# Work moved around the first attention's way through DRAM in a four-layer attention kernel: norms, constants, a late unit and a rounding, with fewer idle products and the fourth layer's constants on ScalarE

## The reference

```python
# layer 0: linear attention over 1500 keys, 16 heads; then layernorm(att @ dense_w + dense_b)
kv = einsum('bhnd,bhne->bhde', k_prime, vh); att = (q' kv) / (q' . sum k')
# ffn 0: quantised (8 bit rows, three-valued weights) silu(gate) * up, down
# layer 1: windowed attention (the 56 first keys, rotary positions), mixture of 16+2 experts
# layer 2: k = l2norm(layernorm(ctx) @ Wk) * k_scale; attention of normalised queries over 1556 keys, 8 heads
#          quantised gelu ffn
# layer 3: attention over 1500 keys, 16 heads, softmax with a row maximum; mixture of 8 experts
```

## Time and profile before

| | |
|---|---|
| three runs, median (lowest to highest) | 840.04 us (837.87 to 840.55) |
| the profiled execution's own time | 838.38 us |
| its span | 836.6 us, mean granted TensorE clock 0.943 |
| PE busy | 747.0 us, 89% of the span |
| DVE busy | 605.0 us, 72% |
| ACT busy | 416.7 us, 50% |
| POOL busy | 321.8 us, 38% |
| chain that ended last | PE 47%, DVE 37%, ACT 5%, POOL 5% |

### The profile page before, as it was taken

The page is one execution under the profiler, slowest core; times in us unless marked ns, Lnnn a source line. Parts: engine busy times, 40 slices in busy tenths (PEclk is TensorE's granted clock), DMA queues, the critical chain, the costliest instruction groups (busy, mean ns, idle before and its releaser), DMA issues.

```text
span 836.6 us, 15735 instructions
## 1 busy us (share of the span) xinstructions
PE 747.0 (89%) x5624; PEld 490.0 (59%) x5624; DVE 605.0 (72%) x1279; ACT 416.7 (50%) x694; POOL 321.8 (38%) x263
## 2 busy tenths in 40 slices
PE   4699999997876969998999999997799998998997
PEld 3577777875544565653455555563246665655575
DVE  4789999998887665557556665568789997535653
ACT  2666666676664524435554545411137776834331
POOL 0665555551423602530778777721251211100111
PEclk9999999999988868999999999998869999998999
DMA  7266766432415312216033322027715667000320
GB/s 204 74 211 244 256 215 214 167 117 94 76 50 175 118 35 81 81 39 165 2 91 108 107 77 77 0 30 109 157 54 107 129 143 151 3 1 26 112 77 24
DMA packets 50338, 87.84 MB, mean 105 GB/s; under 512 B 17386, under 2 KB 34730, under 8 KB 49922
## 3 DMA queue, kind: packets, MB, share of 16 engines
q1 hardware_dynamic: 50274, 86.98, 38.0%
HBM read 61.45 MB, written 25.51 MB: 104 GB/s over the span
## 4 chain that ended last, share of the span: by engine, by line
PE 47%; DVE 37%; ACT 5%; POOL 5%; issue 4%; DMA 1%; SPq 0%; DVEq 0%; POOLq 0%; ACTq 0%
DVE arena L2414 9%; PE ps L1145 8%; PE ps L1135 6%; DVE arena L1810 6%; DVE rn L1962 5%; PE ps L1313 3%; PE ps L1066 3%; DVE arena L2011 3%; PE ps L1323 3%; DVE arena L1990 2%; PE ps L1250 2%; PE ps L750 2%; PE ps L1239 2%; PE ps L1079 2%; DVE arena L1970 2%
## 5 line engine op out<-in xcount | busy, mean ns | idle before, releaser
L1810 DVE TENSOR_TENSOR arena<-ps,arena 128x448 f32<-128x448 f32 (+7 forms) x139 | 82.4, 617 | 57.1 <-ACT arena L1622 20.9
L2414 DVE TENSOR_REDUCE arena<-ps 112x1 f32<-112x500 f32 x192 | 114.6, 669 | 8.8 <-PE ps L1222 8.7
L1747 POOL TENSOR_TENSOR arena<-arena 125x448 f32<-125x448 f32 x96 | 109.2, 1138 | 24.6 <-ACT arena L1567 20.8
L1145 PE MATMUL ps<-arena 125*128 125x448 f32 (+1 forms) x208 | 97.2, 548 | 2.0 <-ACT arena L1567 1.5
L1598 ACT ACTIVATE arena<-ps 125x896 f32<-125x896 f32 x96 | 87.2, 917 | 22.7 <-PE ps L1239 22.7
L1567 ACT ACTIVATE arena<-arena,kbias 125x448 f32<-125x448 f32 x96 | 63.6, 668 | 65.4 <-DVE arena L1810 47.9
L1810 DVE TENSOR_TENSOR arena<-ps,rn 125x448 f32<-125x448 f32 x96 | 59.2, 618 | 48.8 <-PE ps L1135 43.9
L1135 PE MATMUL ps<-arena 128*125 128x448 f16 (+3 forms) x312 | 76.6, 354 | 0.1
L825 PE MATMUL ps<-w_k2h,arena 128*125 128x512 f16 x288 | 67.6, 386 | 8.5 <-ACT arena L1379 8.5
L1135 PEld LDWEIGHTS ps<-arena 128*125 128x125 f16 (+1 forms) x312 | 40.3, 133 | 53.7 <-issue 42.3
L1725 POOL TENSOR_TENSOR arena<-arena 112x512 f32<-112x512 f32 x23 | 29.1, 1267 | 88.9 <-DVE arena L1810 88.7
(11 more groups left out here) (310 smaller groups left out, 1413.8 us busy)
## 6 DMA issues: line engine op xcount, KB each, us to landing
arena<-in_ctxT SPq DMA_DIRECT2D x8, 750.0 KB, 9.4
d_cln<-arena SPq DMA_DIRECT2D x8, 750.0 KB
d_clnT<-arena SPq DMA_DIRECT2D x8, 750.0 KB
d_k<-arena SPq DMA_DIRECT2D x24, 250.0 KB
d_v<-arena SPq DMA_DIRECT2D x24, 250.0 KB
arena<-d_clnT SPq DMA_DIRECT2D x8, 750.0 KB
arena<-in_ctx SPq DMA_DIRECT2D x8, 672.0 KB
arena<-d_cln SPq DMA_DIRECT2D x8, 672.0 KB
```

Of the source, the lines that this page charges most:

```text
L1145: pe.matmul(ps[0:D, 4 + 2 * p, 0:N], cln_s[p][0:rows, t, :], pexp[(t + p) % 2][0:rows], start=(t == 0), stop=(t == KT)).then_inc(l2_pv, 1)
L1747: ins = pool.tensor_tensor(psum2[p][0:rows], psum2[p][0:rows], pexp[(t + p) % 2][0:rows], ALU.add)
L1810: return dve.tensor_tensor(out, a, b, op)
L2414: dve.tensor_reduce(mx3[bn % 2][:, u % 2, u % 8 // 2, u // 8:u // 8 + 1], ps[0:TT, max_bank_of(bn, u), 0:500], AX.X, ALU.max).then_inc(l3_ ...
```

## The change

It moves work, drops some idle products and gives one set of constants to another engine:

- **ScalarE:** unit 10 and `k1T` are taken before the wait for the store; then the squares of ten key tiles and of two more, then the constants, then unit 11, then the last six squares. The root of the norms goes behind units 17 and 18.
- **GpSimd:** multiplies `k1T` by the cosines and adds the sines' part (VectorE makes that part alone), between units 10 and 11; the first two `key_blocks` go behind the first two powers, with a wait for the store instead of `l1_zero`.
- **TensorE:** unit 11 goes behind the projection and two of the key tiles; six tiles remain behind it. A wait for `l1_zero` stands before the first scores.
- **VectorE:** four norms of the last sequence before the turn instead of six, the weights' rounding under the projection, two norms under the second layernorm's power, three and one around the first ffn, two under the queries' product; the clamp `rn_sq` and `key_biases` under the rotation.
- **SyncE:** the wait for `rn_sq` and the loads of units 20 to 23 go from before unit 16's store to unit 19's.
- **Idle products:** 26 become 22 in the second ffn, 14 become 7 and 12 become 6 in the third layer's start.
- **Third layer's start:** the latent keys' sums of squares are made in four pieces, three of them before the copies of the turned queries; their reciprocal goes behind four of the eight subtractions.
- **Fourth layer:** ScalarE sets `v3s` after the third attention (two fills by Identity with scale 0, four small copies) instead of GpSimd's memsets.

```diff
@@ sync
-            sp.wait_ge(rn_sq, 1)
-            for u in range(20, 24):
-                load_later(u)
             for u in range(16, 24):
+                if u == 19:
+                    sp.wait_ge(rn_sq, 1)
+                    for v in range(20, 24):
+                        load_later(v)
                 store_later(u)
@@ tensor
-            later(11)
             pe.wait_ge(l0_att, 3)
             l2_keys(B - 1, 0, 8, range(KT // 2, KT), bank=3)
-            l2_keys(B, 1, 0, range(KT // 2), bank=3)
+            l2_keys(B, 1, 0, range(4), bank=3)
             pe.wait_ge(l0_ld, 32)
             transposes(y2, 2)
             op.next()
             by_tokens(xT2, w_d0[:, :], 0)
-            l2_keys(B, 1, 0, range(KT // 2, KT), bank=3)
+            l2_keys(B, 1, 0, range(4, 6), bank=3)
+            later(11)
+            l2_keys(B, 1, 0, range(6, KT), bank=3)
...
-                    keep_clock(26, 7)
+                    keep_clock(22, 7)
...
+            pe.wait_ge(l1_zero, 3)
             scores1(0)
...
-            keep_clock(14, 3)
+            keep_clock(7, 3)
...
-            keep_clock(12, 2)
+            keep_clock(6, 2)
@@ scalar
+            later(10)
+            act.wait_ge(l1_kv, 1)
+            act.activation(k1T, ps[0:D, 1, 0:N], ACT.Identity, bias=w_col1[:, 1:2]).then_inc(l1_ak, 1)
+            l2_squares(B - 1, 8, range(KT // 2, KT), bank=3)
+            l2_squares(B, 0, range(6), bank=3)
             for p in range(2):
                 act.wait_ge(st[p], 32 * (B // 2 + 1))
...
-            later(10)
-            act.wait_ge(l1_kv, 1)
-            act.activation(k1T, ps[0:D, 1, 0:N], ACT.Identity, bias=w_col1[:, 1:2]).then_inc(l1_ak, 1)
             later(11)
-            l2_squares(B - 1, 8, range(KT // 2, KT), bank=3)
-            l2_squares(B, 0, bank=3)
+            l2_squares(B, 0, range(6, KT), bank=3)
...
+            later(17, 18)
             act.wait_ge(rn_sq, 1)
...
-            later(17, 18, 19)
+            later(19)
...
+            act.wait_ge(l3_free, 1)
+            for p in range(2):
+                act.activation(v3s[p].rearrange("p j n -> p (j n)"), ones[0:KP].broadcast_to([KP, KT * 192]),
+                               ACT.Identity, scale=0.0).then_inc(l3_vz, 1)
+            act.wait_ge(l3_vz, 2)
...
@@ gpsimd
-            remainders(10, 11)
+            remainders(10)
+            pool.wait_ge(l1_kv, 2)
+            ch.link(pool.tensor_tensor(k1T, k1T, cs("cosk"), ALU.mult))
+            pool.wait_ge(l1_k, 1)
+            pool.tensor_tensor(k1T, k1T, xT3, ALU.add).then_inc(l1_k, 1)
+            remainders(11)
...
-            pool.wait_ge(l1_zero, 3)
-            pool.wait_ge(l1_k, 1)
+            rsqrt()
+            rsqrt()
+            for p in range(2):
+                pool.wait_ge(st[p], 32 * (B // 2 + 1))
+            pool.wait_ge(l1_k, 2)
             key_blocks(0)
             key_blocks(1)
-            rsqrt()
-            rsqrt()
             remainders(12, 13, 14, 15, 16)
...
-            for p in range(2):
-                ch.link(pool.memset(v3s[p], 0.0))
...
+            pool.wait_ge(l3_vz, 4)
@@ vector
-            quantised_weights(slice(0, 3))
-
             dve.wait_ge(l1_kv, 2)
-            ch.step(tt(xT3, ps[0:D, 0, 0:N], cs("sink"), ALU.mult))
-            ch.link(tt(k1T, k1T, cs("cosk"), ALU.mult))
-            tt(k1T, k1T, xT3, ALU.add).then_inc(l1_k, 1)
+            tt(xT3, ps[0:D, 0, 0:N], cs("sink"), ALU.mult).then_inc(l1_k, 1)
...
-            l2_norms(B, 0, range(KT // 2))
+            l2_norms(B, 0, range(4))
             turned(xT2, 2)
-            key_biases()
+            quantised_weights(slice(0, 3))
...
-            layernorm(x, z, 1e-5)
+            layernorm(x, z, 1e-5, meanwhile=lambda: l2_norms(B, 0, range(4, 6)))
+            dve.wait_ge(lv_full, 11 - IN_TURNS + 1)
...
-            l2_norms(B, 0, range(9, KT))
-            dve.wait_ge(sq_used, KT * B + SQ)
-            rn_flat = rn[:, :, :, :].rearrange("p b t h -> p (b t h)")
-            dve.tensor_scalar(rn_flat, rn_flat, 1e-24, None, ALU.max).then_inc(rn_sq, 1)
+            l2_norms(B, 0, range(9, 10))
             down(4)
             residual(4, y)
...
             turned(xT, 0)
+            l2_norms(B, 0, range(10, KT))
             product_in.next()
...
+            dve.wait_ge(sq_used, KT * B + SQ)
+            rn_flat = rn[:, :, :, :].rearrange("p b t h -> p (b t h)")
+            dve.tensor_scalar(rn_flat, rn_flat, 1e-24, None, ALU.max).then_inc(rn_sq, 1)
+            key_biases()
...
+            def latent_key_sums(t):
+                act_in.next()
+                ch.step(dve.tensor_reduce(qss[:, 1, H8 * t:H8 * t + H8],
+                                          big3[:, t, :].rearrange("p (h d) -> p h d", h=H8), AX.X, ALU.add))
...
+            for t in range(NT - 1):
+                latent_key_sums(t)
             product_in.next(3)
```

More of the change, by code:

```diff
@@ L481, in build @@
         l3_v = sem("l3_values_spread")
+        l3_vz = sem("l3_values_constants")
         l3_tn = sem("l3_turned_maxima_copied")
@@ L1568, in _ @@
                             .then_inc(l2_p, 1)
+            act.wait_ge(l3_free, 1)
[4 more added lines that the diff above has]
+            for p in range(2):
+                act.copy(v3s[p][:, :, 0:D].rearrange("p j (g c) -> p j g c", c=32)[:, :, :, 24:25],
+                         ones[0:KP].unsqueeze(2).unsqueeze(3).broadcast_to([KP, KT, 4, 1]))
+                act.copy(v3s[p][:, :, D:].rearrange("p j (g c) -> p j g c", c=16)[:, :, :, HD16:HD16 + 1],
+                         ones[0:KP].unsqueeze(2).unsqueeze(3).broadcast_to([KP, KT, 4, 1])).then_inc(l3_vz, 1)
             for t in range(NT):
@@ L1821, in signal, with layernorm @@
                 dve.nop().then_inc(s, 1)
-            def layernorm(src, dst, eps, gain=None, bias=None, twice=False):
+            def layernorm(src, dst, eps, gain=None, bias=None, twice=False, meanwhile=None):
                 for t in range(NT):
@@ L1839, in layernorm @@
                     ch.sync()
+                if meanwhile:
+                    meanwhile()
                 rstd_in.next()
@@ L2127, in _ @@
             dve.tensor_copy(zqT, ps[0:D, 0, 0:256].bitcast(BF16)[:, 0:N]).then_inc(operand, 1)
-            l2_norms(B, 0, range(KT // 2, 9))
+            l2_norms(B, 0, range(6, 9))
             for t in range(NT):
@@ L2313, in _, with latent_key_sums_last @@
                    over(qss[:, 2, H8 * t:H8 * t + H8], [TT, H8, HD8]), ALU.mult).then_inc(operand, 1)
+            def latent_key_sums(t):
+                act_in.next()
+                ch.step(dve.tensor_reduce(qss[:, 1, H8 * t:H8 * t + H8],
+                                          big3[:, t, :].rearrange("p (h d) -> p h d", h=H8), AX.X, ALU.add))
+            def latent_key_sums_last():
+                ch.link(dve.tensor_reduce(qss[:, 1, H8 * (NT - 1):], big3[:, NT - 1, :].rearrange("p (h d) -> p h d", h=H8),
+                                          AX.X, ALU.add))
+                dve.tensor_scalar(qss[:, 1, :], qss[:, 1, :], 1e-24, None, ALU.max).then_inc(to_act, 1)
+            for t in range(NT - 1):
+                latent_key_sums(t)
             product_in.next(3)
@@ L2317, in _ @@
                 ch.step(dve.tensor_copy(qT2[:, :, TT * t:TT * t + TT], ps[0:D, t, 0:N].rearrange("p (c n) -> p c n", c=4)))
-            act_in.next(5)
+            act_in.next(2)
             signal(operand)
-            ch.link(dve.tensor_reduce(qss[:, 1, :], big3.rearrange("p t (h d) -> p (t h) d", h=H8), AX.X, ALU.add))
-            dve.tensor_scalar(qss[:, 1, :], qss[:, 1, :], 1e-24, None, ALU.max).then_inc(to_act, 1)
-            act_in.next()
-            dve.reciprocal(qss[:, 1, :], qss[:, 1, :]).then_inc(l2_kn, 1)
+            latent_key_sums_last()
             for h in range(H8):
@@ L2327, in _ @@
                 ch.step(tt(qtT[:, 1, h, :], ps[0:D, h, 0:N], qtT[:, 0, h, :], ALU.subtract))
-                if h % 4 == 3:
+                if h == 3:
                     signal(operand)
+                    act_in.next()
+                    dve.reciprocal(qss[:, 1, :], qss[:, 1, :]).then_inc(l2_kn, 1)
+            signal(operand)
             def scale2(b, p, t):
```

3 lines of the change are left out of this document (removed).

## The result

The changed kernel took 844.05 us (median of five runs), the kernel before 840.04 beside it: ratio 1.0061, 95% interval 1.004 to 1.0081. The profiled execution took 840.76 (span 839.0) against 838.38 (span 836.6). The forecast was 840.3, with no clear change as the likeliest outcome and 0.34 for slower.

The account below looks back on a forecast made before the run. No engine is saturated; in the first attention's tail each waits for another. Terms +6.8 -1.7 -1.4 -1.0 -0.4 -2.05 = +0.25 on the median 840.04 gave 840.3 us, range 832 to 846.

Parts of the forecast that it names:

- The lead is lost behind unit 11: First attention's tail: variance 3.8 us earlier, but GpSimd's power waits behind unit 11's subtraction, ending at 233.0 against 232.88: +0.1.
- The rounding: Behind the second power: VectorE waits for GpSimd's key blocks and two subtractions, 9.0 us; ends at 250.0 against 243.20, +6.8.
- Norms later: At 258.60: one norm stays of three norms and the clamp before the product, -1.7 us.
- "Nothing" for the late loads: Units 20 to 23 load from some 272.7 instead of 261.00, still 6.3 us before TensorE takes unit 20: no cost.
- "Nothing" for the key sums in pieces: Third layer's start: query copies come 1.8 us later, but the sums end where the single one ended: no cost.
- Idle products: 14 to 7 at the latents' turn -1.4 us, 12 to 6 before the third attention -1.0, 26 to 22 in second ffn -0.4.
- Constants: Second ffn's first scales, 566.37: VectorE's 2.22 us become 0.17 as ScalarE replaces GpSimd's memsets, -2.05.
- The slower rival: Third attention's first two or three tiles take 2.6 us instead of 1.3 at low clock: +2.7, 843 us; chance 0.20.
- The first two rivals: GpSimd doesn't hold VectorE in the rounding: 832 us, chance 0.17; unit 11 doesn't precede the power either: 828, chance 0.06.

Follow-up runs that it names:

- d1: The changed kernel unedited, run again on another chip (the second comparison): 841.37 us against 838.49 for the kernel before, ratio 1.003.
- a2: Changed kernel with GpSimd's first power ahead of unit 11's remainder: 835.68 us against 838.07 for the kernel before, ratio 0.9984.
- a1: Changed kernel with GpSimd's first two key blocks right behind the turned keys: 835.72 us against 838.07 for the kernel before, ratio 0.9972.
- a4: Changed kernel with two key norms in the second layernorm's wait and the clamp before the turned copy: 839.94 us against 838.07 for the kernel before, ratio 1.0025.
- b3: Changed kernel with the latent keys' sums one reduction again, reciprocal ahead of the subtractions: 837.44 us against 837.61 for the kernel before, ratio 1.001.
- b1: Kernel before with only the fourth layer's constants moved to ScalarE, GpSimd's six memsets out: 835.31 us against 837.61, ratio 0.9971.
- b2: Kernel before with only the shorter idle products (14 to 7, 12 to 6, 26 to 22): 836.96 us against 837.61, ratio 0.9984.
- d2: Changed kernel with memsets, 14, 12 and 26 idle products and whole latent key sums put back: 842.56 us against 838.49 for the kernel before, ratio 1.0046.
- d3: Changed kernel with a1, a2, a4, b3 and nine idle products for six before the router's turn: 833.28 us against 838.49 for the kernel before, ratio 0.9935.
- d4: d3 with unit 13 projected with units 14 to 16, behind the first hidden products: 831.33 us against 838.49 for the kernel before, ratio 0.9913.

## Why the prediction was nearly right in its sum and missed the side

The time lies inside the range, 3.75 us above the forecast by the first comparison; by the second, 840.04 times 1.003 is 842.6, 2.3 above.

By the table, the first profile of the changed kernel is 2.4 us longer than the one before, stage by stage: +5.6 to R (forecast +6.8), +0.6 from there to X (-1.7), +0.3 to the latents (-1.4), -1.2 to the attention (-1.0), -0.1 to L1185 (nothing), -2.0 to L1203 (-2.45) and -0.9 in the unchanged end. d1 is 1.0 longer: +4.0, -0.8, -1.1, -0.2, +2.4, -2.2, -1.1. So the large term was forecast too large, the small gains behind it did not all come, and TensorE's clock, at one place in one execution and at another in the next, makes up the rest. That the sum came near was partly luck.

- **The lead is lost behind unit 11**: right in kind, a little small. The power's end was forecast at 233.0 and came at 233.66. a2 shows the cause: the idle goes from 5.55 to 0.20.
- **The rounding** (+6.8): the mechanism was right and a1 shows it; +5.65 in the first profile, and R stands 4.0 and 5.6 us later than before in the two profiles of the changed kernel. The term that was too large is the two subtractions at the end: the forecast had them block for 2.1 us, and they took 0.65 (L1893 at 0.78 and L1891 at 0.21, each 0.17 in a1), since VectorE was in a reduction beside the first of them.
- **Norms later** (-1.7): the first feed-forward's down scaling came 3.86 later than before against 5.65 at the rounding, so -1.8. Right there; at X, by the spread of that stretch, the gain isn't seen.
- **"Nothing" for the late loads**: wrong in the first profile. The lead was as forecast, 6.3 us before TensorE takes unit 20, and 7.1 came of it (from 276.90 to the end of the first scores, 283.96); but the context was there only at 285.34, 8.4 us after the issue. Issuing the four loads took 3.15 us against 1.78 in d1. The DMA engines were busy for 0.70 and 0.94 of the time from 278 to 282, but in d1 for 0.72 and 0.99 from 276 to 280, so their load doesn't explain it. In d1 the same lead was enough, and in a2 5.9 us were. The term lacked a bound for a slow load; with the loads 3.8 earlier (a4) there is no wait.
- **"Nothing" for the key sums in pieces**: wrong, and this is the step that failed in every profile. The forecast saw that the copies of the turned queries come later, but followed only the last sum to its end, and not the copies to TensorE's sixteen products, which they release. It cost 0.5 to 1.7 us (b3).
- **Idle products**: 14 to 7, forecast -1.4. In the kernel before the fourteen took 3.81 us and held up the join; in b1 they took 3.19, and from the sixteen products ahead of them to the latents' copy it was 4.93 us, as with seven (4.94 in the changed kernel; 6.24 before). So the gain is 1.3 where TensorE's clock is low at that spot and nothing where it is full. 12 to 6, forecast -1.0: 1.75 in b2, of which d2 leaves 0.2 where the clock is full. 26 to 22, forecast -0.4: none that shows (44.73 with 26 in d2, 44.72 with 22 in b2; beside ScalarE's constants 42.37 with 26 in b1, 42.18 to 43.27 with 22).
- **Constants** (-2.05): exact in the trace, and 2.3 by b1's medians.
- **The slower rival** (TensorE's clock in the third attention's first tiles, 843) did not occur in the first profile: L1139's first nine products took 2.28, at a granted clock of 1.00 from 401 to 405. There the clock fell one step earlier, on the sixteen products of L1127 (0.53 from 395 to 397), behind the idle that the sums in pieces leave. It did occur in d1, where the loop to L1185 took 2.4 us more against the forecast's 2.7. Of the eleven profiles with six idle products d1 has it in full, d3 and d4 for 0.4 us, and the other eight not at all, so no run shows that fewer idle products bring it. That its 843 is the measured time is luck: the profile nearest its mechanism is the shorter of the two.
- **The first two rivals** (GpSimd doesn't hold VectorE; unit 11 doesn't stand ahead of the power) did not occur. They are what a1 and a2 make true by moving the work.

What stays open is the size: 0.6% and 0.3% in two comparisons. The experts' eight products at the low clock (1.4 to 1.7 us) occur in five of the 14 profiles, b1 among them, which shares its front with the kernel before; they go with the longer waits ahead of them, and no run here ties those to the change. Nor is there a reason on record why the front's variance comes up to 3 us apart in executions of the same code.

## What to carry to other kernels

Work moved off one engine's queue is free only for as long as the stretch it lands in has cover: GpSimd's key blocks cost nothing beside reductions and 5.8 us beside scales. Before moving an operation onto a helper engine, list what that engine must answer quickly (here a power of 1 us that VectorE, and all behind it, waits for), and keep long or late-fed work behind the answer. And follow each piece of a split operation to what stands behind it in the queue, not only to where the last piece ends.

## What was not expected of the hardware

- With both engines' queues full, only VectorE waited: four scales of 0.33 us lasted 1702 to 1844 ns each beside four blocks that stayed at 1687. The forecast had VectorE wait for every block; that the blocks lose nothing is new. Elsewhere one scale waited for two GpSimd operations in a row, as in the earlier trace rows. In a1, at 265 us, the source line of the scales reads:

```profile
L1866 DVE TENSOR_SCALAR arena<-x,arena x4: 333/334/2110, 265.7 to 268.3; 112x128 f32<-112x128 f32 x4
```

- The Trainium skill (SBUF — State Buffer, Who interferes with whom) has the shared pair as an exclusive lock and leaves reductions out of it. The runs agree on the reductions (ten at 0.65 us beside the blocks) and on the scales, which lasted as long as a block. It has issue order decide who blocks. By that alone, scales queued since 238.34 would have gone ahead of the blocks behind the running one, and those would have waited; here each scale waited for a block, and no block took more than 1.687 us.
- The same code, from the masked scores to the end, took 240.7 to 244.8 us over 14 profiles, and one product group of the experts 3.25 or 4.95 us with the granted clock at 1.00 or about 0.56.
